# Score products of a two-layer graph network: the low part of k in both partition halves, and h transposed in the aggregation's space

## What is computed

```python
def _L0_gnn_ref(x, adj, W, b):
    Wi, Wj = (W[:, :Din], W[:, Din:])
    mi = jnp.einsum('bkd,od->bko', x, Wi)
    mj = jnp.einsum('bkd,od->bko', x, Wj)
    a = adj.astype(x.dtype)
    deg = a.sum(axis=1)
    return deg[None, :, None] * (mi + b) + jnp.einsum('ij,bjo->bio', a, mj)

def _L1_gnn_ref(h, adj, ...):          # 8 heads of 64
    q = split_heads(h @ Wq.T + bq)
    k = split_heads(h @ Wk.T + bk)
    v = split_heads(h @ Wv.T + bv)
    scores = jnp.einsum('bhqd,bhkd->bhqk', q, k) * scale
    scores = jnp.where(mask, -jnp.inf, scores)
    attn = jax.nn.softmax(scores, axis=-1)
    out = jnp.einsum('bhqk,bhkd->bhqd', attn, v)
    return out.transpose(0, 2, 1, 3).reshape(b, n, D_MODEL) @ Wo.T + bo

x = _layernorm(x + _L0_gnn_ref(x, adj, L0_gnn_W, L0_gnn_b), axis=-1)
x = _layernorm(x + _L1_gnn_ref(x, adj, ...), axis=-1)
```

## Time and profile before

| | |
|---|---|
| median of 3 runs | 3146.48 us (3145.89 to 3148.19) |
| span of the profiled execution | 3145.9 us; no time of this execution beside its span is told, and the lowest of the runs, 3145.89, is the same to 0.1 |
| TensorE busy | 3097.3 us, 98% of the span, 19456 products |
| VectorE busy | 2451.1 us, 78% |
| ScalarE busy | 1960.7 us, 62% |
| GpSimd busy | 1154.5 us, 37% |
| mean granted TensorE clock | 0.993 of full speed |
| share of the chain that ended last | TensorE 98%, VectorE 1% |
| copies of k_twice | 256 transfers of 128 KB, 2.4 us from issue to landing |

### The profile page before, as it was taken

One profiled execution on the slowest core, in us unless ns is written; L12 is line 12 of the kernel. 1 busy time (PEld: TensorE's weight loads), 2 busy tenths in 40 slices (PEclk: granted clock), 3 DMA queues, 4 the chain that ended last, 5 costly groups with the idle time before them and its releaser, 6 DMA issues.

```text
span 3145.9 us, 59689 instructions
## 1 busy us (share of the span) xinstructions
PE 3097.3 (98%) x19456; PEld 2715.3 (86%) x19456; DVE 2451.1 (78%) x6156; ACT 1960.7 (62%) x4999; POOL 1154.5 (37%) x1097
## 2 busy tenths in 40 slices
PE   6999999999999999999999999999999999999997
PEld 5888888888888888888888888888888888888886
DVE  5778778778778787787787787877877878778776
ACT  3656666666566566666665666666656656666665
POOL 2333333433433333334333333333343333333432
PEclk8999999999999999999999999999999999999999
DMA  4011011111110110111111101111111111011110
GB/s 134 25 51 53 27 53 43 37 53 33 47 53 27 53 53 27 53 36 44 53 32 48 53 27 53 49 31 53 33 47 53 29 51 53 27 53 41 39 48 28
DMA packets 109868, 141.95 MB, mean 45 GB/s; under 512 B 7696, under 2 KB 73744, under 8 KB 109840
## 3 DMA queue, kind: packets, MB, share of 16 engines
q1 hardware_dynamic: 109840, 141.59, 15.2%
HBM read 74.46 MB, written 33.55 MB: 34 GB/s over the span
## 4 chain that ended last, share of the span: by engine, by line
PE 98%; DVE 1%; ACT 0%; issue 0%; DMA 0%; POOL 0%; POOLq 0%; DVEq 0%; SPq 0%
PE proj L349 73%; PE av L349 8%; PE pt L492 7%; PE score L475 4%; PE score L480 3%; PE proj L426 2%; DMA probs<-in_w0T 0%; DVE h L875 0%; DVE k_lo L786 0%; DVE probs L808 0%; DVE pT_lo L823 0%; DVE oT L832 0%; DVE wj_lo L927 0%; DVE wo_lo L927 0%; POOL var_eps_h L284 0%
## 5 line engine op out<-in xcount | busy, mean ns | idle before, releaser
L639 ACT ACTIVATE probs<-probs,exp_bias 128x256 f32<-128x256 f32 x1024 | 509.2, 499 | 247.2 <-DVE exp_bias L814 247.2
L292 POOL TENSOR_TENSOR oT_lo<-oT,oT_hi 128x256 fp32r<-128x256 f32 x256 | 189.8, 742 | 949.3 <-ACT oT_hi L669 949.3
L808 DVE CUSTOM_DVE_ANT_0 probs<-score,mask_add 128x256 f32<-128x256 f32 x1024 | 371.6, 420 | 86.2 <-PE score L480 42.2
L259 POOL TENSOR_TENSOR probs<-probs,row_inv 128x512 f32<-128x512 f32 x256 | 267.0, 1043 | 459.3 <-DVE row_inv L819 459.3
L648 ACT ACTIVATE probs<-probs,row_inv 128x256 f32<-128x256 f32 x512 | 234.2, 509 | 236.9 <-DVE row_inv L819 236.9
L655 ACT CAST pT_hi<-pt 128x512 fp32r<-128x512 f32 x512 | 280.4, 587 | 160.3 <-PE av L349 97.1
L823 DVE TENSOR_TENSOR pT_lo<-pt,pT_hi 128x512 fp32r<-128x512 f32 x512 | 333.5, 681 | 6.1 <-ACT pT_hi L655 0.2
L844 DVE SCALAR_TENSOR_TENSOR h<-proj,deg,xb 128x512 f32<-128x512 f32 x128 | 96.0, 751 | 254.2 <-PE proj L349 254.2
L786 DVE SCALAR_TENSOR_TENSOR q_both<-proj,bq_cols,q_both 64x256 fp32r<-64x256 f32 x512 | 247.6, 484 | 56.3 <-ACT q_both L617 48.7
L349 PE MATMUL proj<-hT_hi,wq_hi 128*128 128x256 f32 x1024 | 289.2, 282 | 1.5 <-DVE hT_lo L764 1.5
L349 PE MATMUL proj<-hT_hi,wq_lo 128*128 128x256 f32 x1024 | 289.0, 282 | 0.0
(11 more groups left out here) (98 smaller groups left out, 8826.6 us busy)
## 6 DMA issues: line engine op xcount, KB each, us to landing
xT_raw<-in_xT SPq DMA_DIRECT2D x64, 512.0 KB, 4.5
xb<-in_x SPq DMA_DIRECT2D x64, 512.0 KB, 5.2
k_twice<-k_twice SPq DMA_DIRECT2D x256, 128.0 KB, 2.4
out<-hb SPq DMA_DIRECT2D x64, 512.0 KB, 3.3
probs<-in_w0T SPq DMA_DIRECT2D x1, 1024.0 KB, 6.8
hb<-in_w0T SPq DMA_DIRECT2D x1, 1024.0 KB, 9.0
probs<-in_wqT SPq DMA_DIRECT2D x1, 1024.0 KB, 5.5
hb<-in_wkT SPq DMA_DIRECT2D x1, 1024.0 KB, 5.8
```

The costliest lines, as they stand in the source:

```text
L259: pool.tensor_tensor(probs[:, g % 2, 1, :, :], probs[:, g % 2, 1, :, :], row_inv[:, g % 2, R:2 * R].unsqueeze(2).to_broadcast([P, R, N]), ...
L292: pool.tensor_tensor(oT_lo[:, g, :], oT[:, :], oT_hi[:, g, :].bitcast(F32), ALU.subtract).then_inc(o_split, 1)
L639: last = nc.scalar.activation(e, e, ACT.Exp, bias=exp_bias[:, g % 2, s:s + 1], scale=SCALE, accum_out=row_sum[:, g % 2, s:s + 1])
L808: last = V.tensor_tensor_reduce(out=probs[:, g % 2, i, r, :], in0=score[i][:, r * N:(r + 1) * N], in1=mask_add[:, r, :], scale=1.0, scalar ...
```

## The change

- `k_lo`, four blocks by pairs of heads, becomes `k_lo_twice`, eight blocks by heads, as large as `k_twice`. VectorE writes the low part of k at home as before (same eight operations), and SP copies it into the other half in the new `copy_k_low`: 4 more transfers of 128 KB per step, each pair behind a wait for VectorE's part (`read["k"]`).
- The third score term becomes a product of full height. Since `q_both` has the low part of q in the other half, it also adds low q times low k, a fourth term. A group is now eight products of 128 rows: for each head and row block `k_twice` and at once `k_lo_twice` into the same place. The end of the even head is signalled after four of them.
- TensorE waits for the new copies before each score group. VectorE waits, before it writes the low part of k, until the scores that read the old one are done.
- `hT_hi` and `hT_lo` are views of `mj_hi` and `mj_lo`.

```diff
-        hT_hi = sb("hT_hi", [P, C, N], F32R)
-        hT_lo = sb("hT_lo", [P, C, N], F32R)
+        hT_hi = mj_hi[:, :, :].rearrange("p r (a n) -> p (r a) n", a=2)
+        hT_lo = mj_lo[:, :, :].rearrange("p r (a n) -> p (r a) n", a=2)
...
-        k_lo = sb("k_lo", [P, C, N], F32R)
+        k_lo_twice = sb("k_lo_twice", [P, HEADS, N], F32R)
...
+            def copy_k_low(n, half):
+                sp.wait_ge(read["k"], 2 * n + half + 1)
+                for i in range(2):
+                    heads = slice(4 * half + i, 4 * half + i + 3, 2)
+                    sp.dma_start(k_lo_twice[(1 - i) * HALF:(2 - i) * HALF, heads, :].bitcast(F32),
+                                 k_lo_twice[i * HALF:(i + 1) * HALF, heads, :].bitcast(F32)).then_inc(
+                                     k_lo_copied[half], 16)
...
                 copy_k(b + 1, 0)
+                copy_k_low(b + 1, 0)
                 copy_k(b + 1, 1)
+                copy_k_low(b + 1, 1)
...
                 pe.wait_ge(k_copied[g // 2], 32 * (b + 1))
+                pe.wait_ge(k_lo_copied[g // 2], 32 * (b + 1))
...
-                blocks = [(i, r) for i in range(2) for r in range(R)]
-                for i, r in blocks:
+                for i in range(2):
                     head = 2 * g + i
-                    pe.matmul(score[i][:, r * N:(r + 1) * N], q_both[:, head, r * P:(r + 1) * P],
-                              k_twice[:, head, :], start=(r == 0), stop=False, skip_group_check=True)
-
-                for i, r in [(i, r) for r in range(R) for i in range(2)]:
-                    head, home = 2 * g + i, slice(i * HALF, (i + 1) * HALF)
-                    last = pe.matmul(score[i][:, r * N:(r + 1) * N], q_both[home, head, r * P:(r + 1) * P],
-                                     k_lo[home, g, :], start=False, stop=True, skip_group_check=True)
-                    if r == R - 1:
-                        last.then_inc(score_done, 1)
+                    for r in range(R):
+                        for k_ in (k_twice, k_lo_twice):
+                            last = pe.matmul(score[i][:, r * N:(r + 1) * N], q_both[:, head, r * P:(r + 1) * P],
+                                             k_[:, head, :], start=(r == 0 and k_ is k_twice),
+                                             stop=(k_ is k_lo_twice), skip_group_check=True)
+                    last.then_inc(score_done, 1)
...
             def k_low_half(n, half):
+                if not (type(n) is int and n == 0):
+                    dve.wait_ge(score_done, 2 * G * (n - 1) + G * (half + 1))
                 biased_low("k", n, half, bk_cols, k_twice,
-                           lambda t, i: k_lo[i * HALF:(i + 1) * HALF, t, :])
+                           lambda t, i: k_lo_twice[i * HALF:(i + 1) * HALF, 2 * t + i, :])
```

More of the change, by code:

```diff
@@ L144, in build @@
         k_copied = [sem("k_copied0"), sem("k_copied1")]
+        k_lo_copied = [sem("k_lo_copied0"), sem("k_lo_copied1")]
         norm_odd_done = sem("norm_odd_done")
@@ L238, in _ @@
             copy_k(0, 0)
+            copy_k_low(0, 0)
             copy_k(0, 1)
+            copy_k_low(0, 1)
             steps(sp, step, lambda b: store(b - 1, 0))
```

## The result

The changed kernel takes 3112.94 us (median of 4 runs, 3112.68 to 3113.30) against 3146.67 (4 runs, 3145.89 to 3148.19): 34 us less, a ratio of 0.9894 with a 95% interval of 0.9882 to 0.9905. The forecast was 3110 with a range of 3103 to 3121. The profiled execution took 3113.12 us with a span of 3111.2; the forecast span was 3110.1.

What follows compares the result with a forecast made beforehand. The prediction took TensorE's pace over its products as the bound. Saving 0.56 us in each of 64 steps, 35.8 us, brought the span from 3145.9 to 3110.1; it forecast 3110 us, range 3103 to 3121.

Steps and rivals of the forecast that it cites:

- The old group, 1.10 and 1.06 us: Old score group on TensorE, stalls included: 1.10 us before 512-wide products (three of four), 1.06 before transposes (one of four).
- The new group, 0.95 us: New score group on TensorE: eight full-height 256-wide products, priced from the av products, 0.95 us without stalls.
- 0.56 us: TensorE's saving per step: 0.15 us for three score groups and 0.11 for one, over 64 steps 35.8 us.
- The costs set at nothing: Low-part copies, new waits on VectorE and TensorE, h transposed in shared space: each claimed to cost nothing.
- The second half of the copies: Second half of k's low part: ready at 1025.4, claimed needed only by the third score group, after 1039.28.
- The margin should stay: At av products of group 2, VectorE's operand was claimed ready 0.45 us early, and that margin to stay.
- Between the last score group and that point TensorE's path loses nothing: Reason given for the kept 0.45 us margin: TensorE saves nothing between the last score group and the av products.
- Rival 1: Score group's stalls, 0.39 us, stay at full height: 0.95 per step more, 61 us slower, 3207; 4%.
- Rival 2: VectorE takes over at the av products: TensorE waits 0.11 per step, 7 us of gain lost, 3117; 8%.

Runs made afterwards that it cites:

- unpaired run: Kernel before with its four half-height products per group reordered so that neighbours use the same half of the array; 3147.36 us, ratio 1.0003.
- late copies: Changed kernel with the copies of the low part of k moved on SP's queue behind the step's store; 3182.57 us.
- run with four pairs: Kernel before with the four half-height products of each score group issued twice; 3205.73 us.
- two switches: Kernel before with each group's products ordered high, high, low, low per row block, one more entry to and exit from half height; 3248.94 us.

## Why the prediction was right

**The old group, 1.10 and 1.06 us.** Right, and its parts are now measured: four full products 0.47, two passes 0.24, 0.39 of stall in four terms, two at each change of height. The prediction read the 0.20 hidden under the followers from 5.79 against 5.59. Whoever had taken the two lines' own rows, 0.47 + 0.43 = 0.90 against 0.96 after, would have forecast the change slower by 15 us.

**The new group, 0.95 us.** It is 0.96, 0.96, 0.95 and 0.95. The followers gave back 0.19, 0.20 and 0.18, the transposes 0.15. A step saves 0.52 and not 0.56: the term "0.56 us" was too large by 0.04, or 2.6 us in 64 steps, by the rounding of rows to 0.01 that the range allowed for.

**The ends.** The steady steps give 62 x 0.52 = 32 us of the 34.7 by which the spans differ. Of the rest, 2.1 us come before the first steady step (the av products ahead of it start at 113.79 before and at 111.67 after), 0.3 in the tail. Some 0.5 of the 2.1 is the saving of the first step's own four groups, and 0.4 a first score group that starts sooner (68.34, from 68.71). Most of what is left is a stretch in which TensorE stayed longer at the lower of its two clock levels (1.2 and 2.4 GHz) in the profiled execution before. The transposes of group 1 there, before and after, in the chain:

```profile
90.05 1.90 PE pt L492 x8
```

```profile
89.24 0.87 PE pt L503 x8
```

That is 1.03 us, 0.15 of it the stall. The granted clock from 68 to 92 us was 0.87 before and 0.93 after. It was 0.93 in the unpaired run too and 0.86 in the run with the views alone, and both are as fast as the kernel before. So I don't count it as the change's; with one profiled execution of each, what sets it isn't shown.

**The time.** The span came out 1.1 above the forecast one (3111.2 against 3110.1): 2.6 too much in the steady steps, and some of it given back in the first. Another 1.9 us lie outside the span (3113.12 for the execution after); I had set span and device time equal, and had dropped the 0.6 that I had just read between them (3146.48 - 35.8 is 3110.7). The 1.1 and the 1.9 are the 3 us by which 3110 was too low. The chances don't add up either: by the rivals they are 92% for faster by more than 6 us, 3% for within it and 5% for slower, where 94, 2 and 4 stand.

**The costs set at nothing.** TensorE's list of waits has none that recurs, so the copies, both new waits and the shared space cost it nothing; the late copies show that the first would once they came 5 us later. The second half of the copies had more cover than I read: 1039.28 is where the second group starts, and the third, which needs them, starts 6.6 us later. "The margin should stay" was wrong: VectorE ended at 1009.26 and av of group 2 started at 1009.61, 0.35 us and not 0.45:

```profile
1007.97 1.29 DVE L837 TENSOR_TENSOR pT_lo<-pt,pT_hi 128x512 fp32r<-128x512 f32 x2
...
1009.61 0.36 PE L364 MATMUL av<-pT_hi,v_both 128*128 128x256 f32 x1
```

Counted from the transposes of h (992.57 in the chain after), VectorE's `pT_lo` starts 15.40, 15.40 and 15.39 us later in the kernel before, the changed one and the run without the third term, while the av products come 17.38, 17.28 and 16.79 later. Score group 3 lies in between. What holds up VectorE longest thus doesn't wait for that group, and what this one group saves (0.11, and 0.58 without the third term) comes off the margin; what the other three save doesn't. The step that failed is "Between the last score group and that point TensorE's path loses nothing": it left out the group's own saving, with the 0.15 under its transposes, which stand right there. It was harmless at 0.10 of 0.45; without the third term 0.58 was more than there was.

Where VectorE loses its tie to group 3 can be seen at its `exp_bias` of that group. It takes 0.17 to 0.50 us for the other groups; here it ends with GpSimd's `xT_lo`. Before, and then after:

```profile
1008.93 1.83 DVE L814 TENSOR_SCALAR exp_bias<-row_max 128x4 f32<-128x4 f32 x1
1008.34 2.40 POOL L265 TENSOR_TENSOR xT_lo<-xT_raw,xT_hi 128x1024 fp32r<-128x1024 f32 x1
...
996.92 1.94 DVE L828 TENSOR_SCALAR exp_bias<-row_max 128x4 f32<-128x4 f32 x1
996.44 2.39 POOL L280 TENSOR_TENSOR xT_lo<-xT_raw,xT_hi 128x1024 fp32r<-128x1024 f32 x1
```

The ends are 1010.76 and 1010.74, 998.86 and 998.83. GpSimd's run of work there starts beside score group 3 and doesn't wait for it (at 1005.36 in the kernel before, released by the inverse sums that VectorE starts at 1005.12). Why VectorE's instruction lasts until GpSimd is done, no run here tests.

**The rivals.** Rival 1 had the sizes right (0.24 of passes, 0.39 of stall) and lost on the point that it turned on: all of the stall went with the half height. Rival 2 named the place; its reason, a VectorE chain that doesn't follow TensorE from batch to batch, isn't what the rows show: the chain keeps its place in the step (15.40) and slips against group 3 alone. The Trainium skill, "TensorEngine Tiling (Array Packing)", has two rules that bear on this. By its Theoretical Speedup, tiles for a contraction of up to 64 run up to twice as fast, and here they do: 0.12 us for a pair against 0.24 for two full products. By its Key Properties, a change of tiling mode drains the engine, and the 0.39 us of stall at the two changes agree with that. Which is larger depends on how many products stand between two changes.

## What to carry to other kernels

Price a small group of products by the starts around it, not by its own rows: a change of height delays two starts on the way in and two on the way out, and half of that stands under the follower's name. Packing two half-height products into one pass saves 0.12 us a pair and the round trip costs 0.39. By an estimate from these two numbers it pays from four pairs in a row on (eight products); the run with four pairs has their price (0.67 + 0.20), but twelve full-height products weren't run beside it. With two pairs, as here, full height with half the rows doing unneeded work is faster. When TensorE is the bound and gets shorter, ask for each of its margins which part of the saving lies between the point from which the other engine's chain runs by itself and the point where its result is wanted. Here that was one score group in four: 0.10 of the 0.52 us saved per step came off the shortest margin, and 0.58 of the 2.2 used it up. Look for such waits under the weight loads as well as under the products.

## What the runs showed of the hardware

- A round trip from full to half height and back costs 0.39 to 0.40 us at the full clock, with 256-wide products in the group (two switches: 102 us for 256 round trips more). Each of the two changes delays the first start after it by 0.09 and the second by 0.10 (kernel before: starts at 1032.78, 1032.99, 1033.21, 1033.42, 1033.76); where the second start is that of a 128-wide transpose it is 0.06 (1.02 for the transposes, 0.87 after).
- The order of four half-height products over two halves made no difference (3147.36 against 3146.52), while four in one half took 0.24 us more. In the unpaired run the third product in program order started 0.2 us before the second.
- After a wait for a transfer the second product started 0.22 us after the first and not 0.12 (late copies, 1040.24 and 1040.46).
- A delay of TensorE by 0.21 us, 62 times, shows as waits of its weight loads and not of its products (run without the third term).
- VectorE's `exp_bias` of group 3 ended within 0.03 us of GpSimd's `xT_lo`, at 1.83 and 1.94 us where it otherwise takes 0.17 to 0.50 (kernel before, changed kernel); the cause is open.
